# A GNN block with eight experts on one core: layernorm, gate and top-2 in three batches over three engines, and the slot table in bf16 parts

## The reference

```
x = x + gnn(layernorm(x), edges, ...)
xf = layernorm(x)
gate_logits = xf @ Wg + bg + bias            # 8 experts
topk_vals, topk_idx = top_k(gate_logits, 2)
topk_w = softmax(topk_vals)
h = relu(xf @ W1[e] + b1[e]);  y = h @ W2[e] + b2[e]
x = x + sum over the two chosen e of topk_w * y
```

## Time and profile before

| what | value |
|---|---|
| median of 3 runs | 1694.28 us |
| lowest, highest | 1693.99, 1695.84 us |
| span of the profiled execution | 1693.0 us |
| TensorE busy | 1461.4 us (86%) |
| VectorE busy | 675.2 us (40%) |
| ScalarE busy | 387.6 us (23%) |
| GpSimd busy | 166.6 us (10%) |
| mean granted TensorE clock | 0.926 |

### The profile page before, as it was taken

One profiled execution on the slowest core, in us unless ns is written; L12 is line 12 of the kernel. 1 busy time (PEld: TensorE's weight loads), 2 busy tenths in 40 slices (PEclk: granted clock), 3 DMA queues, 4 the chain that ended last, 5 costly groups with the idle time before them and its releaser, 6 DMA issues.

```text
span 1693.0 us, 24943 instructions
## 1 busy us (share of the span) xinstructions
PE 1461.4 (86%) x8538; PEld 814.1 (48%) x8539; DVE 675.2 (40%) x1560; ACT 387.6 (23%) x1010; POOL 166.6 (10%) x145
## 2 busy tenths in 40 slices
PE   3564678888889899989999899998999873999996
PEld 2553444444443444535444454534445443566664
DVE  7989777777621220122201230112201357233332
ACT  1220443434401400023001320014000330233332
POOL 1000000000000000000000000000000003466664
PEclk9875899999989999989999899999999876899999
DMA  5153000000000000000000000000004090233433
GB/s 134 38 195 108 1 1 1 1 2 1 14 2 0 14 1 0 1 15 1 0 1 0 14 1 1 1 0 13 1 0 95 7 334 20 52 63 63 66 64 40
DMA packets 49549, 57.87 MB, mean 34 GB/s; under 512 B 14319, under 2 KB 41601, under 8 KB 49184
## 3 DMA queue, kind: packets, MB, share of 16 engines
q1 hardware_dynamic: 38688, 41.67, 8.6%
q0 software_dynamic: 10752, 14.69, 5.4%
HBM read 42.36 MB, written 13.99 MB: 33 GB/s over the span
## 4 chain that ended last, share of the span: by engine, by line
PE 76%; DVE 12%; ACT 5%; issue 4%; DVEq 2%; DMA 1%; POOL 1%; SPq 0%; POOLq 0%; ACTq 0%
PE bank L654 37%; PE bank L735 13%; PE bank L1148 6%; PE bank L1163 6%; ACT at L1618 3%; PE bank L1752 3%; PE bank L1154 1%; PE bank L644 1%; DVE ohL L1409 1%; PE bank L1697 1%; PE bank L738 1%; PE bank L1750 1%; PE bank L1140 1%; DVE ohS L1524 1%; DVEq L505 1%
## 5 line engine op out<-in xcount | busy, mean ns | idle before, releaser
L654 PE MATMUL bank<-at,m 125*128 125x500 fp8e4 (+1 forms) x3500 | 698.8, 356 | 9.4 <-issue 3.1
L654 PEld LDWEIGHTS bank<-at,m 125*128 125x128 f16 x3500 | 319.0, 98 | 345.9 <-issue 39.0
L663 DVE TENSOR_TENSOR aggT<-bank,dinvB 128x500 f32<-128x500 f32 (+1 forms) x70 | 42.2, 620 | 345.8 <-PE bank L654 345.8
L826 ACT ACTIVATE hT<-bank,prm 128x500 f32<-128x500 f32 (+1 forms) x70 | 40.5, 630 | 602.8 <-PE bank L738 602.8
L874 POOL TENSOR_TENSOR idJ<-idJ,wts 125x1400 f32<-125x1400 f32 x2 | 8.0, 4005 | 1406.0 <-DVE idJ L1032 1406.0
L735 PE MATMUL bank<-hT,wcur 128*128 128x500 f32 (+1 forms) x280 | 125.3, 570 | 0.0
L788 DVE BATCH_NORM_STATS2 zst<-hT 128x6 f32<-128x500 f32 (+1 forms) x70 | 40.3, 617 | 199.9 <-ACT hT L826 199.9
L735 PE MATMUL bank<-aggT,wcur 128*128 128x500 f32 (+1 forms) x280 | 116.9, 540 | 0.0
L1148 PE MATMUL bank<-w1s,xtT 128*128 x224 | 109.3, 611 | 0.1
L1163 PE MATMUL bank<-w2s,h1T 128*128 x448 | 106.1, 380 | 1.4 <-ACT h1T L939 1.4
L623 DVE SCALAR_TENSOR_TENSOR m<-bank,dinvP,m 125x256 f16<-125x256 f32 x100 | 48.0, 483 | 148.2 <-ACT m L635 148.2
(11 more groups left out here) (319 smaller groups left out, 1446.7 us busy)
## 6 DMA issues: line engine op xcount, KB each, us to landing
slrow<-sl_dram SPq DMA_DIRECT2D x26, 512.0 KB, 4.8
w1s<-in_L_ffn_W SPq DMA_DIRECT2D x1, 4096.0 KB, 14.2
w2s<-in_L_ffn_W SPq DMA_DIRECT2D x1, 4096.0 KB, 18.9
xin<-in_x SPq DMA_DIRECT2D x1, 2800.0 KB
x<-in_x SPq DMA_DIRECT2D x1, 2800.0 KB
out_rows<-x SPq DMA_DIRECT2D x1, 2800.0 KB
xn_dram<-xn SPq DMA_DIRECT2D x1, 2800.0 KB
wraw<-in_L_gnn_mlp_w SPq DMA_DIRECT2D x5, 512.0 KB, 3.6
```

Of the source, the lines that this page charges most:

```text
L654: last = pe.matmul(bank[banks[g % len(banks)]][:, 0:w], m[:, s, k, h * 128:(h + 1) * 128], at_block(g // H)[:, s, :], start=s == 0 and k = ...
L663: dve.tensor_tensor(aggT[:, h, a:a + w], bank[banks[g % len(banks)]][:, 0:w], dinvB[:, a:a + w], ALU.mult).then_inc(s_agge, 1)
```

## The change

**Three batches.** The 25 tiles go in batches of 8, 8 and 9. VectorE adds and takes statistics for one batch, and makes its `frs` and a shift `fsh` = -mean x frs. ScalarE then writes the batch's `xn` (in place of VectorE), with its copies of `xnT` between. TensorE does the residual transpose of tile t, then the transpose of `xn` tile t - 10, with the gate products and back-transposes of each block in between. Each kind of transpose has two PSUM banks in place of four. `max` and `max_index` are done block by block.

**Slot table in bf16.** `oneJ`, `idJ`, `ohR` and a new `wJ` are bf16, with the two choices side by side as the innermost dimension. The node number is given as tile and place, and the weight as three bf16 parts (`wpart`) whose sum is the f32 weight. VectorE does all multiplications and GpSimd none. TensorE forms ids first (50 products, 112 columns), then weights (50 products, 168 columns). `wJ` lies over `xn`, so VectorE waits for the copy to `xn_dram` before it writes `wJ`. The eight instructions on expert numbers (`cmpJ` to `te`) now follow `rowG` and `rowS`, and `wS` comes last.

```diff
-        ohR = r("ohR", [P, NT, TT], F32)
+        ohR = r("ohR", [P, NT, TT, 2], BF16)
...
-        idJ = r("idJ", [P, 2, NT, 2, J], F32)
+        oneJ = r("oneJ", [P, NT, J, 2], BF16)
+        idJ = r("idJ", [P, NT, 2, J, 2], BF16)
         assert r.at <= w_end
+        r = Region(xn_at)
+        wJ = r("wJ", [P, NT, 3, J, 2], BF16)
...
+        LN_BATCHES = ((0, 8), (8, 16), (16, NT))
+        LN_BANKS = (0, 1)
+        LN_AHEAD = 10
...
         def experts_pool(pool, step):
 
-            for n in range(2):
-                pool.wait_ge(s_place, n + 1)
...
         def experts_act(act):
...
+            for b, (lo, hi) in enumerate(LN_BATCHES):
+                act.wait_ge(s_fve, b + 1)
+                act.activation(fsd[:, lo:hi], fve[:, lo:hi], ACT.Sqrt).then_inc(s_fsd, 1)
+                act.wait_ge(s_frs, b + 1)
+                for t in range(lo, hi):
+                    act.activation(xn[:, t, :], x2[:, t, :], ACT.Identity, scale=frs[:, t:t + 1], bias=fsh[:, t:t + 1]).then_inc(s_fn, 1)
+                    if t >= lo + 2:
+                        turned(t - 2)
+                turned(hi - 2)
+                turned(hi - 1)
...
         def experts_dve(dve, step, rounded, inverse_root):
...
+            for b, (lo, hi) in enumerate(LN_BATCHES):
+                for t in range(lo, hi):
+                    dve.wait_ge(s_oT, t + 1)
+                    dve.tensor_tensor(x2[:, t, :], x2[:, t, :], bank[LN_BANKS[t % 2]][0:P, 0:D], ALU.add).then_inc(s_oTe, 1)
+                    if t > lo:
+                        statistics(t - 1)
+                step(statistics(hi - 1))
...
+                inverse_root(frs[:, lo:hi], fve[:, lo:hi], fsd[:, lo:hi], ft1[:, lo:hi])
+                dve.scalar_tensor_tensor(fsh[:, lo:hi], fmv[:, lo:hi, 0], -1.0, frs[:, lo:hi], ALU.mult, ALU.mult).then_inc(s_frs, 1)
...
+            for q, (a, w) in enumerate(COLS):
+                lo, hi = a // P, (a + w) // P
+                dve.wait_ge(s_gate, q + 1)
+                dve.tensor_copy(lgt[:, lo:hi, :].rearrange("p t e -> p (t e)"), bank[6 + q % 2][0:P, lo * NE:hi * NE]).then_inc(s_lgt, 1)
...
+            step(dve.tensor_copy(wpart[:, 0, :, :], pair))
+            step(dve.tensor_tensor(wrem[:, 0, :, :], pair, wpart[:, 0, :, :], ALU.subtract))
...
+            step(dve.tensor_tensor(oneJ[:, :, :, :], iotaJ2[:, :, :].unsqueeze(1).to_broadcast([P, NT, J, 2]), along(slkey[:, 0, :, :], J), ALU.is_equal))
+            dve.tensor_scalar(idJ[:, :, 0, :, :], oneJ[:, :, :, :], iotaX[0:P, 1:2], None, ALU.mult)
+            dve.tensor_tensor(idJ[:, :, 1, :, :], oneJ[:, :, :, :], along(iotaN2[:, :, :], J), ALU.mult).then_inc(s_idJ, 1)
...
+            dve.wait_ge(s_xnd, 32)
+            for k in range(3):
+                last = dve.tensor_tensor(wJ[:, :, k, :, :], oneJ[:, :, :, :], along(wpart[:, k, :, :], J), ALU.mult)
+            last.then_inc(s_wJ, 1)
+            dve.wait_ge(s_idw, 1)
+            step(dve.tensor_copy(placeJ[:, :], bank[2][:, 0:J]))
+            step(dve.scalar_tensor_tensor(idsJ[:, :], bank[2][:, J:2 * J], float(P), placeJ[:, :], ALU.mult, ALU.add))
...
+            dve.wait_ge(s_idw, 2)
+            dve.tensor_reduce(wS[:, :], bank[3][:, 0:3 * J].rearrange("p (k j) -> p j k", k=3), axis=XYZ, op=ALU.add).then_inc(s_tab, 1)
...
         def experts_pe(pe):
-            for t in range(NT):
+            def residual(t):
...
+            def rows_up(t):
+                pe.wait_ge(s_fn, t + 1)
+                if t >= 2:
+                    pe.wait_ge(s_gTe, t - 1)
...
+                done = t + 1
+                if done % (CQ // P) == 2 and done > CQ // P:
+                    gates(done // (CQ // P) - 1)
+                if done % (CQ // P) == 0 and done > CQ // P:
+                    back(done // (CQ // P) - 2)
+
+            for t in range(NT):
+                residual(t)
+                if t >= LN_AHEAD:
+                    rows_up(t - LN_AHEAD)
+            for t in range(NT - LN_AHEAD, NT):
+                rows_up(t)
+            gates(NQ - 2)
+            gates(NQ - 1)
+            back(NQ - 2)
+            back(NQ - 1)
...
+            for s_moving, moving, out_b, width in ((s_idJ, idJ, bank[2], 2 * J), (s_wJ, wJ, bank[3], 3 * J)):
+                pe.wait_ge(s_moving, 1)
```

More of the change, by code:

```diff
@@ L280, in gnn_ffn_program @@
         nte = r("nte", [P, 4, NE], F32)
-        slf = r("slf", [P, 2, NT], F32)
-        sltile = r("sltile", [P, 2, NT], F32)
-        slplace = r("slplace", [P, 2, NT], F32)
+        slf = r("slf", [P, NT, 2], F32)
+        sltile = r("sltile", [P, NT, 2], F32)
+        slround = r("slround", [P, NT, 2], F32)
+        slkey = r("slkey", [P, 2, NT, 2], BF16)
+        wpart = r("wpart", [P, 3, NT, 2], BF16)
+        wrem = r("wrem", [P, 2, NT, 2], F32)
+        placeJ = r("placeJ", [128, J], F32)
+        idsJ = r("idsJ", [128, J], F32)
         pad = r("pad", [128, J], F32)
@@ L919, in experts_act @@
                 act.wait_ge(s_gT, t + 1)
[L920 removed]
+                act.activation(xnT[:, q % 2, :, t % per * P:(t % per + 1) * P], bank[2 + t % 2][:, 0:H * P].rearrange("p (h n) -> p h n", h=H), ACT.Copy).then_inc(s_gTe, 1)
                 if q == 1 and t % per == 0:
@@ L957, in experts_dve @@
             dve.wait_ge(s_x2, 32)
[L958 to L974, removed]
-                dve.tensor_scalar(xn[:, t, :], x2[:, t, :], fmv[:, t, 0:1], frs[:, t:t + 1], ALU.subtract, ALU.mult).then_inc(s_fn, 1)
@@ L977, in experts_dve, with statistics @@
-            dve.wait_ge(s_cst, 2)
-            dve.wait_ge(s_gate, 1)
-            step(dve.tensor_copy(lgt[:, :, :].rearrange("p t e -> p (t e)"), bank[6][0:P, 0:NT * NE]))
-            for t in range(NT):
-                last = dve.max(top[:, t, :], lgt[:, t, :])
-            step(last)
-            for t in range(NT):
-                last = dve.max_index(tix[:, t, :], top[:, t, :], lgt[:, t, :])
+            per = CQ // P
+            def statistics(t):
+                dve.wait_ge(s_oTe, t + 1)
+                return dve.bn_stats(fst[:, t, :], x2[:, t, :])
@@ new lines, in experts_dve @@
+            for b, (lo, hi) in enumerate(LN_BATCHES):
[5 more added lines that the diff above has]
+                step(statistics(hi - 1))
+                for t in range(lo, hi):
+                    last = dve.bn_aggr(fmv[:, t, :], fst[:, t, :])
+                step(last)
+                dve.tensor_scalar(fve[:, lo:hi], fmv[:, lo:hi, 1], LN_EPS, None, ALU.add).then_inc(s_fve, 1)
+                dve.wait_ge(s_fsd, b + 1)
+                inverse_root(frs[:, lo:hi], fve[:, lo:hi], fsd[:, lo:hi], ft1[:, lo:hi])
+                dve.scalar_tensor_tensor(fsh[:, lo:hi], fmv[:, lo:hi, 0], -1.0, frs[:, lo:hi], ALU.mult, ALU.mult).then_inc(s_frs, 1)
+                if b == 0:
+                    dve.wait_ge(s_fw, FW)
+                    dve.tensor_tensor(gbs[:, :], gbr[:, 0:1], gbr[:, 1:2], ALU.add).then_inc(s_gbs, 1)
```

125 lines of the change are left out of this document (60 added, 65 removed).

## The result

| | before | after |
|---|---|---|
| median | 1694.13 us | 1674.97 us |
| lowest, highest (4 runs each) | 1692.62, 1695.84 us | 1671.07, 1675.79 us |
| span of the profiled execution | 1693.0 us | 1669.4 us |
| VectorE, ScalarE, GpSimd busy | 675.2, 387.6, 166.6 us | 670.7, 400.7, 155.0 us |

The ratio is 0.9878, with a 95% interval of 0.9861 to 0.9894: 19.2 us less between the medians, against 21.3 forecast (the rounded 1673; the terms added to 21.6).

What follows compares the result with a forecast made beforehand. No engine was full between the last normalisation and the first expert product; the engines take turns. Gate 4.8, table 13.3 and first experts' clock 3.5 sum to 21.6 us, from 1694.28 to 1672.7, so 1673; range 1668 to 1686.

Steps and rivals of the forecast that it cites:

- Gate: Stage from ScalarE's last GNN normalisation (its start is S) to the last index: three batches gain 4.8 us.
- at the high clock: Third batch: TensorE's seven tiles of two pairs take 3.2 us, two gate blocks 3.7 us, at 2.4 GHz.
- upper bound of 6.8: Gate gain in us if TensorE's clock is high from the start, 2 us more than the 4.8 forecast.
- half low: Clock low for about half of the gate stage, falling at each batch start: 1683 us in total, chance 0.08.
- wpart hidden: The five instructions for wpart, 1.0 us, lie in the 1.20 us in which VectorE waits for the ranks.
- Copy: Copy to xn_dram, queued behind w2: complete near 1412.4, no VectorE wait ahead of wJ, 0.7 us to spare.
- Masks: VectorE's table multiplications at the 16-bit rows' rate: oneJ 1.6, ohR 3.6, wJ 4.8 us.
- The rival of half rate: Broadcast inner pairs keep VectorE's table multiplications from the rows' rate: 11.6 us more, 1685 us in total, chance 0.05.
- Weight products: The table's 50 TensorE products of 168 columns take 6.0 us, starting at the low clock and rising; bounds 3.8 to 7.5.
- Clock of the first experts: TensorE runs the first expert products at 2.4 GHz instead of half rate: 3.5 us gained, bounds 0 and 4.1.
- The handshake rival: Hops between engines with two banks slow each batch tile: 1698 us, deciding at 1.0 us per tile, chance 0.03.
- The page's rule: Transposes don't count as TensorE being busy, so the clock stays low through the gate: 1690 us, chance 0.12.

Runs made afterwards that it cites:

- two experiments: Filler products in TensorE's batch gaps plus idJ's first half on ScalarE, against the kernel after: 1671.33 us; the same with the xn_dram copy issued first: 1668.91 us.
- two edits: Each against the kernel after: filler products in TensorE's gaps at the batch starts, 1674.11 us; first half of idJ computed on ScalarE, 1670.71 us.

## Why the prediction was right, and where its terms were off

- **Gate, 4.8 predicted, 3.96 measured.** The way was right: start of the mixed work 11.0 us behind S (11.4 forecast), last index at 50.28 (49.4). The step that failed is "at the high clock" for the third batch: I let the clock rise once and stay. It fell at both batch starts, each time after a gap of TensorE, for 3.2 us in all. That the total missed by 0.9 only is in part luck. From the start of the mixed work to the second batch's `xn` I had 11.7 us, and it took 9.3; from there to the third batch's 11.1, and it took 13.5; the tail 15.2, and it took 16.5. With the gaps filled the gain is 54.24 - 46.87 = 7.4, somewhat above my upper bound of 6.8; so the rest of the schedule was a little pessimistic. The rival "half low" was the right mechanism at a smaller price.
- **wpart hidden.** Right: 9.04 us from index to slots, as before.
- **Copy.** No wait, as forecast, but the room was about 3 us and not 0.7. Of the 2.1 us between, 1.4 are that `wJ` could start only 68.7 us behind S (67.3 forecast), for the later index and the slow `idJ`. The rest is the copy, through by 65.8 us behind S (66.6 forecast); 0.7 was also a slip, since its own terms, 1377 + 29.4 + 5, add to 1411.4 and not 1412.4. The tail of 5 us was about right: w2 left the queue at 1372.33, 29.4 us on is 1401.7, and traffic ended by 1408. Behind the slots the order of transfers decides only once the compute gets 3 us faster, as two experiments then showed.
- **Masks.** `oneJ` 1.62 (1.6), `ohR` 3.62 (3.6), `wJ` 4.66 (4.8), `rowG` done 14.6 us behind the slots (14.3). The rival of half rate is refuted, but for one instruction: `idJ` took 1.67 where the `tensor_scalar` rate gave 1.0, for its output in 25 runs. That put 0.6 us into the chain, one of the two misses behind the 22.27 us from slots to first `up` (21.1 forecast).
- **Weight products, 6.0 predicted, 6.66 measured**, the other miss. The clock stayed at 0.50 until 1421, to within 1.3 us of their end. In other executions with the same table products they took 5.39 to 6.70, so a size of 6.0 can't be called wrong by this one. With TensorE kept busy before them they took 3.96 (bound: 3.8).
- **Clock of the first experts, 3.5 predicted, 3.95 measured**, and shown by the filled gap in the kernel before.
- **The handshake rival** is refuted: within a batch TensorE's pairs follow each other by 0.42 us at the low clock (1354.16, 1354.59 in its timeline), with no gap at each tile. In the last batch, where TensorE has only `xn` tiles left, there are such waits, for ScalarE, but of 0.3 us, far from the 1.0 at which the rival decides:

```profile
1382.51 0.40 PE L1150 MATMUL bank<-ident,xn 125*128 125x125 f32 x2 [0.25 <-ACT xnT L929]
...
1383.27 0.40 PE L1150 MATMUL bank<-ident,xn 125*128 125x125 f32 x2 [0.35 <-ACT xnT L929]
```

- **The page's rule.** The mixed work of the first batch began with transposes alone. From 1353.16 to the first gate product at 1357.72 TensorE did nothing else, and in this stretch its pairs fell from 0.64 to 0.39 us, at 1356.66: the clock went to 2.4 GHz before there was a product. The Trainium skill, in "TensorE: Matmul & The Clock Gate", Part 4 on the PE-mode transpose, says that transposes do not count as TensorE being busy in the same way; this trace does not agree with it. Why the clock stayed at 0.50 through 13 us of the same transposes in the earlier trace rows stays open: there they came at 0.28 us each (46 in 13.00 us) and all from `hT`, here at 0.21 and from `hT` and `xn` in turn, and no run varied either alone.

## What to carry to other kernels

A gap of TensorE also costs time behind it when its clock falls: the two gaps in the batches, 5.0 us together, came with 3.2 us more in the work behind them. A short stage between long gaps may never reach the high level: the table's weight products took 6.66 us, and 3.96 with filler ahead of them. Look at the clock in the stage behind each gap, and fill the gap or move work into it. Before adding up gains, ask what had room only because the compute was slow: here two edits worth 4.4 and 2.5 us from S to the end gave 3.0 together, and 5.0 once a copy was issued earlier. Ask of each gain which instructions it lies in: 1.1 us of both 4.4 and 2.5 were the same weight products. And measure a stage from a mark in the same execution when what lies ahead of it moves by more than the effect.

## What the runs showed of the hardware

- VectorE's `tensor_scalar` on 2,800 bf16 values takes 0.95 us into a contiguous output and 1.67 into 25 runs of 112; `tensor_tensor` takes 1.61 to 1.62 us either way.
- After gaps of 1.04 and 0.60 us of TensorE, close together, the clock fell under the first expert (first `up` 3.51 us); with 5 filler products in the first gap and a wait of 0.50 left, it did not (1.98 us).
- The part ahead of S, the same in all kernels but for a few constants, varied by 6.8 us between profiled executions (1342.16 to 1348.94).
